# Conditional loads for empty units, and other waits before the first units, in an attention and routed-FFN kernel

## Time and profile before

| | us |
|---|---|
| median of 3 runs | 844.15 (843.95 to 845.01) |
| the profiled execution | 846.81 |
| its span, first to last instruction | 845.1 |
| mean granted clock of TensorE | 0.970 |
| units' scatters, first start to last with rows | 457.9 to 806.3 |
| output copies issued from | 808.8 |

### The profile page before, as it was taken

The page is one execution under the profiler, slowest core; times in us unless marked ns, Lnnn a source line. Parts: engine busy times, 40 slices in busy tenths (PEclk is TensorE's granted clock), DMA queues, the critical chain, the costliest instruction groups (busy, mean ns, idle before and its releaser), DMA issues.

```text
span 845.1 us, 19794 instructions
## 1 busy us (share of the span) xinstructions
PE 744.0 (88%) x5232; PEld 678.8 (80%) x5232; DVE 698.6 (83%) x2401; ACT 572.8 (68%) x1174; POOL 581.7 (69%) x581
## 2 busy tenths in 40 slices
PE   4999999999999999999968798888979897989671
PEld 3899999999999999999857787777778777878661
DVE  5989999999999999999996788778868787878661
ACT  4877778777778777787615687676757676767540
POOL 1056777777677777776776677777777777777753
PEclk9999999999999999999997999999999999999985
DMA  6245544556445544433338999999999999999988
GB/s 178 69 158 202 206 155 166 200 184 216 174 147 198 184 157 147 144 123 117 114 134 275 297 352 309 328 337 333 342 319 319 323 348 325 330 331 338 332 267 271
DMA packets 142317, 199.66 MB, mean 236 GB/s; under 512 B 16752, under 2 KB 117760, under 8 KB 142208
## 3 DMA queue, kind: packets, MB, share of 16 engines
q1 hardware_dynamic: 111152, 113.41, 43.0%
q0 software_dynamic: 28064, 81.93, 25.2%
q10 hardware_dynamic: 2992, 3.06, 1.2%
HBM read 104.19 MB, written 105.04 MB: 248 GB/s over the span
## 4 chain that ended last, share of the span: by engine, by line
PE 46%; DMA 17%; DVE 16%; issue 9%; POOL 6%; SPq 3%; ACT 1%; DVEq 1%; ACTq 0%; POOLq 0%
PE bank_a L319 21%; PE bank_x L319 10%; PE bank_y L319 9%; DMA xn<-rows_by_expert 8%; DMA rows_by_expert<-xn,f_id 7%; DVE xn L1291 3%; POOL rows_by_expert L587 3%; PE bank_a L1495 3%; DMA x_in<-rows_by_expert 3%; DVE hs_l L1304 2%; POOL rows_by_expert L498 2%; PE bank_a L1334 1%; SPq L326 1%; SPq L438 1%; DVE w L1270 1%
## 5 line engine op out<-in xcount | busy, mean ns | idle before, releaser
L587 POOL DMA_INDIRECT rows_by_expert<-xn,f_id x256 | 249.8, 976 | 85.6 <-issue 50.6
L498 POOL DMA_INDIRECT rows_by_expert<-xn,slots_now x192 | 197.2, 1027 | 103.1 <-issue 44.3
L721 ACT CAST xt_h<-bank_a 128x512 fp32r<-128x512 f32 x143 | 84.0, 587 | 68.2 <-PE bank_a L1495 63.2
L1273 DVE TENSOR_TENSOR xt_l<-bank_a,xt_h 128x512 fp32r<-128x512 f32 x143 | 98.1, 686 | 23.9 <-ACT xt_h L721 23.4
L319 PE MATMUL bank_y<-ws,hs_h 128*128 128x256 f32 x512 | 96.4, 286 | 0.5 <-DVE hs_l L1029 0.5
L504 POOL DMA_INDIRECT rows_by_expert<-xn,slots_now x64 | 80.7, 1260 | 17.9 <-issue 14.2
L319 PE MATMUL bank_x<-xt_h,ws 128*128 128x512 f32 x256 | 92.0, 400 | 0.1
L752 ACT ACTIVATE hid<-bank_x 128x256 f32<-128x256 f32 x143 | 55.0, 384 | 53.9 <-PE bank_x L319 44.7
L319 PEld LDWEIGHTS bank_y<-ws,hs_h 128*128 128x128 f32 x512 | 82.6, 192 | 4.0 <-DVE hs_l L1029 0.7
L319 PE MATMUL bank_y<-ws,hs_l 128*128 128x256 f32 x256 | 73.2, 286 | 0.0
L319 PE MATMUL bank_y<-we,hs_h 128*128 x284 | 63.5, 316 | 10.9 <-DVE hs_l L1304 7.1
(11 more groups left out here) (287 smaller groups left out, 2429.6 us busy)
## 6 DMA issues: line engine op xcount, KB each, us to landing
xn<-rows_by_expert SPq DMA_DIRECT2D x204, 272.0 KB, 4.8
x_in<-rows_by_expert SPq DMA_DIRECT2D x71, 272.0 KB
rows_by_expert<-spare SPq DMA_DIRECT2D x22, 544.0 KB, 5.4
x_in<-in_L_attn_x_dram SPq DMA_DIRECT2D x16, 512.0 KB, 4.0
out_dram<-rows_by_expert SPq DMA_DIRECT2D x8, 1024.0 KB, 14.9
rows_by_expert<-xn,f_id POOLq DMA_INDIRECT x286
rows_by_expert<-xn,slots_now POOLq DMA_INDIRECT x256
xn<-rows_by_expert ACTq DMA_DIRECT2D x11, 272.0 KB, 6.6
```

The lines of the kernel that those rows point to most:

```text
L498: G.indirect_dma_start(out=half_rows[:, :], in_=xn[:, c % NB, s, 0:RW], in_offset=None, out_offset=bass.IndirectOffsetOnAxis(ap=slots_now[ ...
L587: G.indirect_dma_start(out=half_rows[:, :], in_=f_y[u % YB][:, tile], in_offset=None, out_offset=offset).then_inc(added[u % CLS], 16)
L721: S_.copy(f_h[u % 4], A[u % 2][:, :].rearrange("p (c s t) -> p c s t", c=KD, s=2)).then_inc(fx_hi, 1)
L1273: V.tensor_tensor(f_l[u % 4], A[u % 2][:, :].rearrange("p (c s t) -> p c s t", c=KD, s=2), f_h[u % 4].bitcast(F32), ALU.subtract).then_inc ...
```

## The change

- Loads of rows and of sums from unit 128 on get a condition, `row > SPARE`; a unit without rows is not loaded. Its buffers then hold an earlier unit's values. Two VectorE steps make `gone` and `below`: for a unit past the last real one the bound for the tag is so high that all its rows count as not to be stored.
- Four of the eight buffers of sums move from the last batch's part of `xn` to other places (`k_f`, `q_f`, `spare`, `x_in`). Sums 4 to 6 are loaded before rows 7. The wait for all scatters of batch 15 now stands before rows 8; sums 5 wait for VectorE to be done with `q_f`.
- SyncE starts when `table` is copied (`table_ready`), not when the expert words are packed. TensorE turns the table's columns first and signals twice.
- Expert words are read one at a time, the next one every six units. The table is read when an entry is first needed; the entries for the end are read before the waits of line 451.
- `upto` is made in batch 14, in another part of `x_in`.
- TensorE runs the down product of unit 0 before turning rows 2, and that of unit 1 before turning rows 3.
- GpSimd's two waits in the scatters begin at unit 10 instead of 6.

Cut to the changed lines; one hunk that repeats `next_experts` for TensorE is left out:

```diff
@@ -222,7 +222,7 @@
 
-        upto = reused(x_in, (E, E), XB * SUB * D - E * E)
+        upto = reused(x_in, (E, E), (XB - 1) * SUB * D - E * E)
         ends = reused(k_f, (E, E), E * E)
@@ -249,7 +249,9 @@
         RB = 8
-        f_y = [reused(xn, (2, RW), (i + 4) % 8 * 2 * RW) for i in range(YB)]
+        f_y = [reused(xn, (2, RW), (i + 4) * 2 * RW) for i in range(4)]
+        f_y += [reused(k_f, (2, RW)), reused(q_f, (2, RW), KD * S - 2 * RW), reused(spare, (2, RW)),
+                reused(x_in, (2, RW), 4 * 2 * RW)]
         f_rows = [reused(xn, (2, RW), (YB + i) * 2 * RW) for i in range(4)]
@@ -258,6 +260,8 @@
         f_none = sb("f_none", [P, YB, 2], U32)
+        gone = sb("gone", [P, E])
+        below = sb("below", [P, E])
         w2 = sb("w2", [P, 4, 2])
@@ -291,8 +295,8 @@
         added = [sem(f"added{i}") for i in range(CLS)]
-        plan_step, zeros_stored, plan_made, plan_turned, plan_ready = sems(
-            "plan_step", "zeros_stored", "plan_made", "plan_turned", "plan_ready")
+        plan_step, zeros_stored, plan_made, plan_turned, table_ready, plan_ready = sems(
+            "plan_step", "zeros_stored", "plan_made", "plan_turned", "table_ready", "plan_ready")
         rows_loaded = [sem(f"rows_loaded{i}") for i in range(RB)]
@@ -322,16 +326,25 @@
         def four_from(engine, i, u, low, high):
-            if u % 4 == 0:
-                fours[engine, i] = fours.get((engine, i), ())[-4:] + nc.values_load_multi_w_load_instructions(
-                    table[i:i + 1, u // P, u % P:u % P + 4], engines=[engine], min_val=low, max_val=high,
+            first = u - u % 4
+            known = fours.get((engine, i), {})
+            if first not in known:
+                known = {n: four for n, four in known.items() if n == first - 4}
+                known[first] = nc.values_load_multi_w_load_instructions(
+                    table[i:i + 1, u // P, first % P:first % P + 4], engines=[engine], min_val=low, max_val=high,
                     skip_runtime_bounds_check_because="the plan makes every entry, and makes it within these bounds")[1]
-            return fours[engine, i][-4 + u % 4]
-
-        def load_experts(engine):
+                fours[engine, i] = known
+            return known[first][u % 4]
+
+        def load_experts(engine, word):
             return nc.values_load_multi_w_load_instructions(
-                packed, engines=[engine], min_val=0, max_val=(1 << 4 * PACK) - 1,
+                packed[:, word:word + 1], engines=[engine], min_val=0, max_val=(1 << 4 * PACK) - 1,
                 skip_runtime_bounds_check_because="each word holds PACK expert numbers of four bits")[1]
+
+        def next_experts(words, engine, u):
+            u += 4
+            if u % PACK == 0 and u < UNITS:
+                words += load_experts(engine, u // PACK)
 
@@ -410,7 +423,7 @@
                 sp.wait_ge(added[k], PRIMED)
-            sp.wait_ge(plan_ready, 1)
+            sp.wait_ge(table_ready, 1)
 
@@ -425,32 +438,46 @@
                     sp.sem_inc(rows_whole, 1)
-                sp.dma_start(f_rows[u % RB], unit_rows(row, 0)).then_inc(rows_loaded[u % RB], 16)
+                if u == EARLY:
+                    sp.wait_ge(scattered[(B - 1) % NB], scatters_until(B - 1))
+                if u < SKIPPED:
+                    sp.dma_start(f_rows[u % RB], unit_rows(row, 0)).then_inc(rows_loaded[u % RB], 16)
+                else:
+                    sp.dma_start(f_rows[u % RB], unit_rows(row, 0), cond=row > SPARE).then_inc(rows_loaded[u % RB], 16)
 
             def load_sums(u):
-                if u == 4:
-                    sp.wait_ge(scattered[(B - 1) % NB], scatters_until(B - 1))
+                if u == 5:
+                    sp.wait_ge(q_lo, B)
                 if u >= YB:
...
                     sp.sem_inc(sums_free, 1)
-                sp.dma_start(f_y[u % YB], unit_rows(row_of.pop(u), 1)).then_inc(acc_loaded[u % YB], 16)
+                row = row_of.pop(u)
+                if u < SKIPPED:
+                    sp.dma_start(f_y[u % YB], unit_rows(row, 1)).then_inc(acc_loaded[u % YB], 16)
+                else:
+                    sp.dma_start(f_y[u % YB], unit_rows(row, 1), cond=row > SPARE).then_inc(acc_loaded[u % YB], 16)
 
...
                     load_set(SH + E - 1)
+                if u == EARLY - 1:
+                    for v in range(EARLY // 2, EARLY - 1):
+                        load_sums(v)
                 if u < UNITS:
                     load_rows(u)
-                if 0 <= u - (ROWS_AHEAD - SUMS_AHEAD) < SUMS_BY_ACT:
-                    load_sums(u - (ROWS_AHEAD - SUMS_AHEAD))
-
+                v = u - (ROWS_AHEAD - SUMS_AHEAD)
+                if 0 <= v < EARLY // 2 or EARLY - 1 <= v < SUMS_BY_ACT:
+                    load_sums(v)
+
+            all_units = [four_from(mybir.EngineType.SP, 2 + k, UNITS, PRIMED, PRIMED + 32 * UNITS) for k in range(CLS)]
             for u in range(SUMS_BY_ACT - CLS, UNITS - 9):
...
             for k in range(CLS):
-                sp.wait_ge(added[k], four_from(mybir.EngineType.SP, 2 + k, UNITS, PRIMED, PRIMED + 32 * UNITS))
+                sp.wait_ge(added[k], all_units[k])
                 sp.sem_inc(sums_free, 1)
@@ -515,6 +542,12 @@
                     scatter_row(c - 2, 11)
+                if c == B - 2:
+                    pool.wait_ge(attn_ready, SUB * (B - 2))
+                    G.memset(upto, 1.0).then_inc(const_step, 1)
+                    pool.wait_ge(const_step, 6)
+                    G.affine_select(out=upto, in_=upto, compare_op=ALU.is_ge, fill=0.0, base=0,
+                                    pattern=[[-1, E], [1, E]], channel_multiplier=0).then_inc(consts_made, 1)
                 if c >= 1:
@@ -529,12 +562,6 @@
                     scatter_row(last, 5)
-                if c == B - 1:
-                    pool.wait_ge(attn_ready, SUB * (B - 1))
-                    G.memset(upto, 1.0).then_inc(const_step, 1)
-                    pool.wait_ge(const_step, 6)
-                    G.affine_select(out=upto, in_=upto, compare_op=ALU.is_ge, fill=0.0, base=0,
-                                    pattern=[[-1, E], [1, E]], channel_multiplier=0).then_inc(consts_made, 1)
                 if c + 1 < B:
@@ -577,7 +604,7 @@
                 for tile in range(2):
-                    if u >= 6:
+                    if u >= 10:
                         if tile == 0:
@@ -739,14 +766,15 @@
                     act.sem_inc(sums_free, 1)
-                act.dma_start(f_y[u % YB], unit_rows(row, 1)).then_inc(acc_loaded[u % YB], 16)
-
-            experts = load_experts(mybir.EngineType.Activation)
+                act.dma_start(f_y[u % YB], unit_rows(row, 1), cond=row > SPARE).then_inc(acc_loaded[u % YB], 16)
+
+            experts = list(load_experts(mybir.EngineType.Activation, 0))
             for u in range(2):
...
             for u in range(UNITS):
+                next_experts(experts, mybir.EngineType.Activation, u)
                 act.wait_ge(fu_done, u + 1)
@@ -1248,8 +1276,12 @@
             hidden_low(SH * B - 1)
+            plan(V.tensor_scalar(gone[:, :], order[:, :], unit_end[:, 0:1], float(SKIPPED + E - 1), ALU.add, ALU.is_le))
+            planned()
+            V.tensor_scalar(below[:, :], gone[:, :], float(2 * WHOLE), 1.0, ALU.mult, ALU.add)
             dve.wait_ge(plan_turned, 1)
-            V.tensor_copy(table, X[0][0:COLS, 0:UR].rearrange("p (j u) -> p j u", j=2))
+            V.tensor_copy(table, X[0][0:COLS, 0:UR].rearrange("p (j u) -> p j u", j=2)).then_inc(table_ready, 1)
+            dve.wait_ge(plan_turned, 2)
             plan(V.tensor_tensor(experts_f, X[1][0:1, 0:WORDS * PACK].rearrange("p (w k) -> p w k", k=PACK),
@@ -1261,7 +1293,7 @@
             dve.wait_ge(plan_ready, 1)
-            experts = load_experts(mybir.EngineType.DVE)
+            experts = list(load_experts(mybir.EngineType.DVE, 0))
 
@@ -1279,8 +1311,8 @@
                 if u >= SKIPPED:
-                    V.tensor_scalar(f_none[:, u % YB, :], onward, 1.0, float(NOWHERE), ALU.is_lt, ALU.mult
-                                    ).then_inc(none_ready, 1)
+                    V.tensor_scalar(f_none[:, u % YB, :], onward, below[:, u - SKIPPED:u - SKIPPED + 1], float(NOWHERE),
+                                    ALU.is_lt, ALU.mult).then_inc(none_ready, 1)
                     dve.wait_ge(none_ready, u - SKIPPED + 1)
@@ -1297,6 +1329,7 @@
                     sum_up(1)
+                next_experts(experts, mybir.EngineType.DVE, u)
                 if 1 < u and u + 2 < UNITS:
@@ -1478,12 +1511,11 @@
             pe.wait_ge(silu_done, SH * B)
-            for j in range(2):
-                T_.matmul(X[0][0:COLS, j * P:(j + 1) * P], u_tab[:, j, :], ident[:, :],
-                          start=(j == 0), stop=True, skip_group_check=True)
-                last = T_.matmul(X[1][0:1, j * P:(j + 1) * P], u_tab[:, j, 1:2], ident[:, :],
-                                 start=(j == 0), stop=True, skip_group_check=True)
```

(12 more changed lines are left out.)

1 line of the change is left out of this document (added).

## The result

The kernel after takes 840.05 us (median; 837.78 to 842.87), the kernel before 844.72 in the same runs. The ratio is 0.9947, with a 95% interval of 0.9935 to 0.9959: faster by 4.7 us, or 0.53%. The forecast was 834.8 us, 9.4 us faster, with a range that ended at 839.5. The sign was right and the size about twice too large. Rival (a), 837.0, is nearer, but the cause it names (a late landing of batch 15, or DMA engines that can't follow) isn't what the trace shows.

A forecast was written before the change was run, and what follows sets the result against it. GpSimd's scatter issue was taken as the limit, DMA engines nearly a second, then the output copies as the end. Start 2.8 plus end 6.6 made 9.4 us off the 844.15 median: 834.8 us, range 829.5 to 839.5.

The forecast's parts named there:

- Rival (a): Batch 15's scatters land 2.6 us late or DMA engines cannot follow GpSimd; start 0.6, end 6.6, 837.0 us; chance 0.22.
- The end, forecast 6.6: Output copies after 808 us: seven unloaded sums, 1.95 MB at the stretch's 297 GB/s, take 6.6 us off.
- 9.2 if the copies alone run at 326 GB/s: Upper bound of the gain at the output copies: 8.39 MB in 25.7 us of today's 34.9.
- The start, forecast 2.8: First units: 2.04 from TensorE's stall plus 0.8 from the low clock, kept from unit 10 on; bounds 0.6 to 8.3.
- The table ahead: SyncE's first loads come 1.35 us earlier, but in series with its wait for the scatters, adding nothing.
- Batch 15's landing: Last routing scatters before rows 7: 0.8 us sooner to 2.6 later possible, taken as 0.35 later.
- the term of 2.04: TensorE near 470 us: its 2.39 us wait for rows 8 goes, 0.35 comes back before rows 7.
- The late thing thereafter is TensorE's own work: Early units: once the 2.39 us stall at rows 8 goes, TensorE's own work is what comes late.
- Rows 12 stand behind a weight set that VectorE finishes after unit 5, so they move along: SyncE's rows 12, issued at 477.44 us, shift earlier together with the units before them.
- the term of 0.8: TensorE's low clock after its stall, 0.66 granted over 470 to 475 us, goes: worth 0 to 1.6, taken as 0.8.
- What stays is that product's shift: GpSimd's gate at unit 10 waits for unit 11's product, so the gain there is its shift, 2.8 us.
- Rival (d): Unit loop: single word reads cost 2.2 us on each of three engines, adding 92 us, 927 us; chance 0.03.

The follow-up runs named there:

- set_at_16: Kernel after, plus a maximum with 0 on table values waited against, with the last weight set loaded behind rows 15 instead of 11: 838.13 us.
- before_bounded: Kernel before with only a maximum with 0 added on table values that a queue waits against: 845.0 us, 1.0014 of the kernel before.

## Why the prediction was wrong

**The end, forecast 6.6, measured 3.0 ± 1.9 and 3.5 ± 2.0.** The mechanism was right in the main: 2 loads are left of ScalarE's 11, the copies end earlier, and the condition on the rows is worth nothing that shows. The step that failed is the term of 1.95 MB "at the 297 GB/s of that stretch". I took the sum of all bytes by all time as the price of each. The loads' bytes cost 3.5/1.90 = 1.8 us per MB in the trace (1.6 by the copies' own end), not 3.4, because the copies are the slow part of the mixture: in the same kind of window they alone run at 282 GB/s (the row from 807.97 us above), the mixture at 297. (The other 297 above, for copies alone, is by packet time and not by window.) That they are slower without loads is measured; why is not known. The bound "9.2 if the copies alone run at 326 GB/s" was on the wrong side of it: alone they run slower than the mixture. The forecast also took the copies for the end of the kernel before. GpSimd's drain was, by 0.6 to 1.0 us in the traces with the empty loads, and the forecast had no term for it; it went away only since the same conditions let the empty units end earlier. The forecast said that no long row shows how fast copies go alone; it should then have asked for the case in which they are slower, and taken a price under 6.6 as likely as one above. This is the largest single error, 3.3 of the 4.7 us between forecast and result.

**The start, forecast 2.8, measured 1.0 to 1.4 by times and 1.6 by traces, each barely or not clear of nothing.** Point by point:
- The constant in batch 14: hidden, as forecast, and gone from GpSimd's row of scatters.
- The table ahead: relative to the plan's last step, the first load of rows came 1.41 us earlier (1.35 forecast). Undone, it costs 0.5 ± 1.8: "in series with SyncE's wait and adds nothing" holds.
- Batch 15's landing, forecast 0.35 later: rows 7, which wait for it, went out 6.79 us behind the issue of the last routing scatter, before 7.77. It was 1.0 sooner in this pair, not later. But in the four traces with the old start the same distance is 6.7 to 8.2, so a shift of 1 us either way isn't shown. By the Trainium skill's rule ("DMA: Bandwidth & Descriptors", Queues, rings and completion order) the sums would have held these scatters back; this trace doesn't show it.
- Rows 8 within 1 us of rows 7, and no stall at rows 8: right.
- "The late thing thereafter is TensorE's own work": this is the first step that failed, and with it the term of 2.04. Rows 7, behind three loads of sums in their own queue, took 5.70 us to land and TensorE stood 1.55 for them. The three loads were priced only as a delay to the scatters, never as one to rows 7.
- "Rows 12 stand behind a weight set that VectorE finishes after unit 5, so they move along": this is the second step that failed. The set depends on VectorE's work, which moved by less than SyncE did; rows 12 were 0.5 us earlier (1.7 counted from batch 0), SyncE stood 5.5 us for the set where it stood 0.7 before, and TensorE's stall there was 2.02 instead of 1.23. set_at_16 takes that stall away. The low clock came at 480 instead of 470, so the term of 0.8 for it wasn't gained in this trace; the one stretch of low clock that it was read from isn't there in before_bounded, which has its own at 480.
- "What stays is that product's shift": right as a rule, and the product of unit 11 shifted by less than forecast: unit 10's scatter came at 488.73, before at 488.95, which is 0.2 us earlier, or 1.5 counted from batch 0.
- Word reads in the loop: 24 on each engine with medians of 0.29 to 0.32 us, and GpSimd without gaps for them. Rival (d) has nothing for it.

The batches start at different times: GpSimd's first inverse root is at 30.2 to 33.0 us in the 20 traces. In the first pair of profiles that hid 1.2 us of the start's gain; the profile before was also 2.7 us above its median. Sums of small terms at the start were below what one profile can tell.

## What to carry to other kernels

When a transfer is removed from beside another, don't price it at the mixture's bytes per time: the two kinds can have quite different prices, and the one that remains may be the slow one. Ask what the remaining one does alone. When a step is moved earlier on a queue, follow that queue to the next wait on something that hasn't moved; here, in the traces, a weight set's place took back a part of it. Ask also what ends just behind the thing that is made shorter: GpSimd's empty units were within 1.4 us of the copies. And an instruction that issues a large transfer can itself be long when others stand ahead of it: four copies of 1 MB held ScalarE's queue for 15 us, so they belong on a queue with nothing behind them.

## What the runs showed that was not expected

- DRAM-to-DRAM copies in packets of 1 KB take 54 ns a packet and engine on one queue, 297 GB/s, and are no faster on two. They begin at 375 GB/s and fall to 278. With loads to SBUF beside them the total is up to 380 GB/s and the copies' own packet time falls to 50 ns.
- The issue of a copy of 1 MB takes 0.7 us for the first two and up to 7.5 for later ones: 14.94 us for four on ScalarE, 20.3 us for eight on SyncE, where a load of 272 KB takes 0.37 us to issue.
- The span can end with a drain of GpSimd's queue, 6.8 us behind the start of its last scatter with no copies left (845.59 to 852.4) and 9.1 us with copies beside (828.21 to 837.3).
- A load whose condition is false leaves the queue in 0.1 us, against 0.4 for one that is done, and moves no bytes.
